# One broadcast DMA of eight rows in place of eight DMAs of one row, in a three-stage perceiver kernel

## The reference, cut to what matters

```
x = x + xattn(layernorm(x), ctx_4096)                    # (2,128,2048) x (2,2048,2048), fake-quantised
x = x + attn(layernorm(x), Wq, Wkv, Wo)                  # ... @ Wo at its end
wq = qweight[:, None, :] >> shifts[None, :, None] & MASK # 256 packed rows -> 2048 rows
zq = unpack4(qzeros) + 1
W = scales[g_idx] * (wq - zq[g_idx])                     # scales: (16, 2048), g_idx = row // 128
x = x + layernorm(x) @ W + bias
```

## Time and profile before

| | us |
|---|---|
| median of 3 runs | 435.19 |
| lowest, highest | 433.32, 437.91 |
| profiled execution | 433.4 |
| its span in the trace | 431.7 |
| TensorE busy (matmuls) | 379.1 (88%) |
| VectorE busy | 323.9 (75%) |
| ScalarE busy | 220.6 (51%) |

### The profile page before, as it was taken

How to read it: one execution, slowest core, us unless ns; L and a number is a source line. 1 busy time by engine, 2 the same in 40 slices (tenths; PEclk the granted TensorE clock), 3 DMA queues, 4 the chain that set the end, 5 groups by cost and what they waited for, 6 DMA issues and landing times.

```text
span 431.7 us, 4679 instructions
## 1 busy us (share of the span) xinstructions
PE 379.1 (88%) x1830; PEld 280.0 (65%) x1836; DVE 323.9 (75%) x316; ACT 220.6 (51%) x266; POOL 38.0 (9%) x75
## 2 busy tenths in 40 slices
PE   0296768776999999999999999999689999999996
PEld 0121322324888877877878868887468878888884
DVE  4699888769842794773955946896999899999922
ACT  2968988986144585474763925412725233444000
POOL 8995000000000000000000001000000000000000
PEclk9998898998999999999999999999699999999999
DMA  7999999994263443535255414999800000000022
GB/s 279 425 424 420 420 421 424 419 390 176 70 222 111 131 162 106 188 102 186 103 183 207 155 40 173 282 201 243 313 2 2 2 0 0 2 0 2 0 97 97
DMA packets 24274, 77.44 MB, mean 179 GB/s; under 512 B 1626, under 2 KB 1802, under 8 KB 19210
## 3 DMA queue, kind: packets, MB, share of 16 engines
q1 hardware_dynamic: 24092, 77.01, 50.0%
q10 hardware_dynamic: 160, 0.13, 0.1%
HBM read 74.91 MB, written 2.10 MB: 178 GB/s over the span
## 4 chain that ended last, share of the span: by engine, by line
PE 70%; DVE 10%; DMA 10%; ACT 7%; issue 3%; SPq 0%; DVEq 0%; ACTq 0%
PE bank L1131 20%; PE bank L1004 12%; PE bank L1006 12%; PE bank L1005 12%; DMA ctx_more<-in_ctx 5%; DMA raw<-in_L_attn_Wo 4%; ACT q L423 4%; PE bank L965 2%; PE bank L1066 2%; PE bank L1091 2%; PE bank L997 2%; DVE q L683 2%; DVE stats L601 2%; PE bank L1079 1%; PE bank L1034 1%
## 5 line engine op out<-in xcount | busy, mean ns | idle before, releaser
L445 ACT ACTIVATE w_hi<-raw 128x2048 fp32r<-128x2048 f32 x29 | 55.3, 1911 | 49.3 <-DMA raw<-in_L_attn_Wo 28.2
L631 DVE TENSOR_TENSOR w_lo<-raw,w_hi 128x2048 fp32r<-128x2048 f32 x29 | 66.2, 2286 | 13.4 <-ACT w_hi L445 13.4
L1004 PE MATMUL bank<-w_hi,xt_hi 128*128 128x512 f32 x128 | 52.0, 406 | 0.0
L965 PE MATMUL bank<-q,at 128*128 128x512 bf16 x122 | 37.4, 429 | 16.3 <-DVE q L683 15.5
L1006 PE MATMUL bank<-w_hi,xt_lo 128*128 128x512 f32 x128 | 50.0, 391 | 0.0
L1005 PE MATMUL bank<-w_lo,xt_hi 128*128 128x512 f32 x128 | 49.9, 390 | 0.0
L1004 PE MATMUL bank<-w_hi,hd_hi 128*128 128x512 f32 x104 | 42.2, 406 | 5.6 <-DVE w_lo L631 5.6
L683 DVE TENSOR_SCALAR q<-q 128x2048 bf16<-128x2048 uint8 x32 | 38.7, 1226 | 6.6 <-ACT q L423 4.6
L1005 PE MATMUL bank<-w_lo,hd_hi 128*128 128x512 f32 x104 | 41.4, 398 | 0.0
L1006 PE MATMUL bank<-w_hi,hd_lo 128*128 128x512 f32 x104 | 41.2, 397 | 0.0
L469 ACT ACTIVATE work<-work,neg_mx 128x128 f32<-128x128 f32 x64 | 24.7, 387 | 23.4 <-DVE neg_mx L798 23.4
(11 more groups left out here) (153 smaller groups left out, 675.7 us busy)
## 6 DMA issues: line engine op xcount, KB each, us to landing
raw<-in_ctx SPq DMA_DIRECT2D x16, 1024.0 KB, 18.1
ctx_more<-in_ctx SPq DMA_DIRECT2D x16, 1024.0 KB, 17.8
raw<-in_L_attn_Wq SPq DMA_DIRECT2D x16, 1024.0 KB, 5.0
raw<-in_L_attn_Wo SPq DMA_DIRECT2D x13, 1024.0 KB, 5.1
raw_fifth<-in_L_attn_Wo SPq DMA_DIRECT2D x3, 1024.0 KB, 7.3
resid<-in_x SPq DMA_DIRECT2D x2, 1024.0 KB, 11.9
scale<-in_L_ffn_scales SPq DMA_DIRECT2D x16, 128.0 KB, 14.0
packed<-in_L_ffn_qweight SPq DMA_DIRECT2D x2, 1024.0 KB, 19.9
```

Source lines behind the costliest of these rows:

```text
L445: nc.scalar.activation(hi_slots[s], raw_slots[s], ACT.Copy).then_inc(w_hi_set, 1)
L631: nc.vector.tensor_tensor(lo_slots[s], raw_slots[s], hi_slots[s].bitcast(F32), ALU.subtract).then_inc(w_lo_set, 1)
L965: mm(bank[:, 4 * b + n, :], at[:, k, b * P:(b + 1) * P], q16[:, i % 2, n * CH:(n + 1) * CH], start=start, stop=False)
L1004: mm(bank[:, out_bank, :], x_hi, hi[:, c], start=first, stop=False)
```

## The change

For each half the loop over eight groups, each with a DMA of one row of `scales` to sixteen partitions, becomes one DMA whose source is walked as eight rows, each repeated sixteen times, and whose destination is all 128 partitions. DVE's wait is for 16 in place of 128. Bytes, destination and the place in SP's queue are the same.

```diff
             for h in range(HALVES):
                 load_granule(wo_rows, W_O, W_O + 11 + h)
-                for i in range(GROUPS // HALVES):
-                    g = h * (GROUPS // HALVES) + i
-                    sp.dma_start(scale[i * PER_GROUP:(i + 1) * PER_GROUP, h, :],
-                                 scales[g:g + 1, :].to_broadcast([PER_GROUP, D])).then_inc(scales_loaded[h], 16)
+                rows = scales[h * (GROUPS // HALVES):(h + 1) * (GROUPS // HALVES), :]
+                sp.dma_start(scale[:, h, :],
+                             rows.unsqueeze(1).to_broadcast([GROUPS // HALVES, PER_GROUP, D])
+                             ).then_inc(scales_loaded[h], 16)
...
-                dve.wait_ge(scales_loaded[h], 16 * (GROUPS // HALVES))
+                dve.wait_ge(scales_loaded[h], 16)
```

## The result

| | before | after |
|---|---|---|
| median of 4 runs | 435.81 | 445.80 |
| lowest, highest | 433.32, 437.91 | 444.62, 446.47 |
| ratio, 95% interval | | 1.0272, 1.0232 to 1.0312 |
| span of the profiled execution | 431.7 | 444.5 |

The kernel is 2.7% slower. By the ratio that is about 11.8 us (10.1 to 13.6); the two medians, of four runs each, differ by 10.0 (2.3%, just under that interval). Against the later medians of the kernel before (434.5 to 435.5) it is 10.3 to 11.3. The forecast was 442.3 us, a rise of 7.1, with a range of 433.5 to 448.0: direction and range hold. The time is 3.5 us above the forecast, next to rival C (445.1), and the rise is too small by 2.9 us (medians) to 4.7 us (ratio).

What follows compares the result with a forecast made beforehand. The prediction took granule 13's landing, followed by DVE's row of work, to bound the kernel. Half 0 +3.8 and half 1 +3.3 made 7.1 us, added to the median 435.2: 442.3 us, range 433.5 to 448.

Steps and rivals of the forecast that it cites:

- rival C: Broadcasts: wherever the other eight engines work a row takes 0.92 us; +9.9 us, 445.1 us; chance 0.18 with beyond.
- What bounds the kernel: Before the transposes: the end moves one for one with granule 13's landing, through DVE's row of work.
- DVE's floor of 4.7 us: DVE's work before granule 13 could end at 298.5 in place of 303.17, so at most 4.7 us gained.
- Eight engines: The new DMA is dealt out by its outermost count: eight shares of sixteen rows on eight engines, none on the others.
- The destination is the limit, 0.61 us a row: New DMA: writes into neighbouring partitions slow it; 0.61 us a row, middle of 0.31 and 0.92, 9.8 us a half.
- The other eight engines, half 0: Free engines' next transfers crowd half 0 for 7.8 us at 0.76 us a row; 11.3 us, +3.8.
- Half 1: Second broadcast: only granule 15 and packed half 1 are left, coming late, so no crowding; 9.8 us, +3.3.
- A gain (A in the chances): Granule 13 reaches ACT before 301; a gain under 1% unless it reaches DVE's floor; chance 0.06.
- B: Broadcasts: eight engines together get the 143 GB/s of sixteen, so it cancels; 435 to 439 us; chance 0.27.
- D: Broadcasts: the DMA is dealt to sixteen engines, 2.6 us a half; 4.7 us gained, 430.5 us; chance 0.04.
- TensorE's clock: TensorE's longer stand: twelve matmuls at half speed, about 5 us, still fit before granule 14 arrives; nothing added.
- The signs: DMA share 0.5 to 0.7, ACT on granules 12 and 13 near 296 and 308, DVE waiting, TensorE standing about 10 us.

Runs made afterwards that it cites:

- one_row_all: Against the kernel before, each half's broadcast is one DMA of a single row to all 128 partitions, seven groups in eight of the scales wrong; 0.9915, 431.33 us.
- early_rows: Against the kernel before, the sixteen old DMAs are issued before granule 8 of Wo, DVE's order unchanged; 0.9909, 431.43 us.
- the probe: A kernel without the computation, ten stages of transfers each timed from issue to landing; plain 1 MB 4.97 us, new DMA alone 11.51 us.
- early_one: Against the kernel before, the two new DMAs are issued before granule 8 of Wo in place of the sixteen old ones; 1.0022, 435.22 us.
- four_rows: Against the kernel before, each half is loaded by two DMAs of four rows in place of eight of one row; one run, 453.76 us.

## Why the prediction was right, and where its size was off

*What bounds the kernel:* right. The landing of granule 13, DVE's row of work from there, the transposes and the end moved by 12.84, 12.83, 12.86 and 12.8 us. DVE's floor of 4.7 us is borne out too: with granule 13 landed early, DVE is busy without a gap up to it in one_row_all, and one_row_all and early_rows gained 3.7 and 4.0 us, with 4.7 inside both intervals. Granule 15, which the chain of waits names, again has 1.9 us of slack in the kernel after (its upper part is there at 324.54, DVE takes it up at 326.47).

*Eight engines:* right, by the 240 packets. The prediction had said that no row showed such a DMA; this is the row.

*The destination is the limit, 0.61 us a row:* right. Alone in the probe it is (11.51 - 2.4) / 16 = 0.57 us a row, in early_one 0.60. From the rows, the middle between the two bounds was a guess, and it came out close. Why eight engines that write sixteen partitions apart get just this rate no run shows.

*The other eight engines, half 0:* **mis-sized.** The step took 0.76 us a row, "midway between 0.61 and 0.92", for the 7.8 us in which the free engines would do three transfers at full speed, and 0.61 behind that: 11.3 us. The middle was a choice between two values; no run shows into which partitions the free engines write. Measured 15.04 - 2.6 = 12.4 us, so the term is off by 1.1 us. What failed is the 7.8 us. The free engines run at about a third of that speed (the estimate from the windows above), the share stays at 1.02 from 285 to 295, and so the crowding lasts for the whole half: 12.4 / 16 = 0.77 us a row, which is the 0.76 of the step, for all sixteen rows. Rival C has the same 12.4 from other parts, 0.92 for 7.8 us and 0.61 for the rest; that it agrees is luck, since in C too the free engines would have been out of work for the last third.

*Half 1:* **the larger error.** The step said "In half 1 only granule 15 and packed half 1 are left for them and come late: I leave it at 9.8." Measured 14.89 - 2.6 = 12.3 us, again 0.77 us a row. The free engines did have work here: share 0.97 at 153 GB/s from 299 to 311. The order of SP's issues says which, packed half 0 and granules 14 and 15, left over since the free engines are slow and the issues late. Term off by 2.5 us. With half 0 in its old form half 1 took 10.5 us, so the term as written is off by 0.7 us there, and the other 1.8 come from what the new half 0 leaves behind it.

The sum with these two terms is 7.1 + 1.1 + 2.5 = 10.7 us. Granule 11 itself landed 0.7 us later (284.13 - 282.02, less the 1.44 from before), which gives the 11.4 of the trace, beside 10.0 to 11.8 measured. That 0.7 is not shown to be the change's: from its issue to ACT granule 11 takes 11.19 us after and 10.52 before, and between 8.7 and 11.8 in the other kernels that keep it in this place.

A gain (A in the chances) is out by the time, and so is B (439 us at the most); D is out by the packets too. *TensorE's clock:* as said, nothing is added to the time. The half speed shows in both traces: behind the 4.13 us of standing the granted clock is 0.52 from 305.5 to 310.5 in the kernel before, and the twelve matmuls fill 4.99 us; in the kernel after it is 0.50 in the long stand (311 to 315) and behind it (318.35 to 323.6), the first matmul takes 0.79 us and the twelve 5.25. They still end 0.51 us before granule 14's can start at 324.35, and the transposes wait for DVE. *The signs:* DVE waits for the scales in both halves, as said. "A DMA share near 0.5 to 0.7" was wrong, for the same reason as the two terms. ACT's starts on granules 12 and 13 came at 299.17 and 314.06, where 296 and 308 were said, and TensorE's standing is 3.35 + 10.36 = 13.7 us in place of about 10.

## What to carry to other kernels

Count how many rows a DMA's source is walked as at its outermost before you merge small DMAs into one, and count the small packets after. Here eight rows, each repeated sixteen times, went to eight engines, four rows to four, and sixteen or 128 rows to sixteen (packets under 512 B: 1386 with two DMAs of eight rows, 1386 with four of four, 1626 with sixteen of sixteen, 1402 with two of 128), and where they wrote at a time set how fast (12.43 us against 21.93). The DMA on eight engines was dearer in a busy queue than alone (5 us against 1.4 more than the eight old ones in the probe): the next transfers crowd it, which takes 15.20 us in place of 11.51, and the last of them lands after 22.39 us in place of 17.62. Look, too, at what the engines that it leaves free will do: if they are slowed as well, the crowding lasts as long as the DMA does (share 1.02 at 156 GB/s beside half 0 here). And when transfers stand in the way, look for the last use of the tile under them: the same sixteen DMAs, issued 25 us earlier and with their DVE work, made the kernel 2.1% faster (1.7 to 2.4).

## What the runs showed of the hardware

- One row of HBM read for 128 partitions by one DMA landed in 4.68 us, a plain 1 MB load in 4.97: the broadcast was not slow in itself.
- Eight DMAs in a row, each into sixteen neighbouring partitions, went at some 140 GB/s, with one row read or sixteen (139 and 143 in the earlier trace rows, 1 MB in 10.10 and 10.03 us less 2.4 in the probe). The correction's loads, also sixteen partitions wide, went at 101. Eight engines writing four partitions apart were 1.8 times as fast as sixteen apart (12.43 and 21.93 us for 2 MB).
- Most issues on SP took 0.4 to 0.8 us (0.39 a granule, 0.73 the new DMA in the kernel after), and some far longer with much work outstanding: up to 10.78 us for one granule here, 15.35 us for the packed half in four_rows. No run shows the cause.
- Transfers of SP's queue landed in the order of their issue: half 0, granule 12, half 1 and granule 13 at 296.31, 299.17, 311.64 and 314.06 in the kernel after.
- Engines that have no part in a DMA were slowed beside it: next to the new one the eight free ones moved about 70 GB/s (an estimate from 156 GB/s in all), where half of 402 would be 201.
